# Two graph attention passes: ScalarE takes a share of the weighting of gathered rows

## The reference, cut to what matters

```python
def gatv2(x, src, dst, Wl, bl, Wr, br, att, bias, heads, out_ch):
    xl = (x @ Wl + bl).reshape(n, heads, out_ch)
    xr = (x @ Wr + br).reshape(n, heads, out_ch)
    e = jax.nn.leaky_relu(xl[src] + xr[dst], 0.2)
    score = jnp.einsum('ehc,hc->eh', e, att)
    smax = jax.ops.segment_max(score, dst, num_segments=n)
    ex = jnp.exp(score - smax[dst])
    denom = jax.ops.segment_sum(ex, dst, num_segments=n)
    alpha = ex / (denom[dst] + 1e-16)
    return jax.ops.segment_sum(xl[src] * alpha[:, :, None], dst, num_segments=n) ... + bias
x = gatv2(embed, ..., heads=4, out_ch=32)
x = jax.nn.relu(x)
return gatv2(x, ..., heads=1, out_ch=128)
```

## Time and profile before

| | us |
|---|---|
| median of three runs | 7670.53 |
| profiled execution, its own time | 7667.1 |
| span of the profiled execution | 7665.4 |
| passes 2 and 3, first gather to last add | 1126.9 and 1114.6 |
| pass 1, first gather to last add | 1079.1 |

### The profile page before, as it was taken

How to read it: one execution, slowest core, us unless ns; L and a number is a source line. 1 busy time by engine, 2 the same in 40 slices (tenths; PEclk the granted TensorE clock), 3 DMA queues, 4 the chain that set the end, 5 groups by cost and what they waited for, 6 DMA issues and landing times. The chain is left out here.

```text
span 7665.4 us, 88585 instructions
## 1 busy us (share of the span) xinstructions
PE 4650.8 (61%) x25719; PEld 3975.8 (52%) x25719; DVE 5099.6 (67%) x13667; ACT 1077.1 (14%) x3113; POOL 4877.5 (64%) x5168
## 2 busy tenths in 40 slices
PE   0444445566664467777567777776656677666665
PEld 0344443455553355555355555665555567555554
DVE  4333334577777788888688888647777754777776
ACT  0333332000000111111111111110000011000001
POOL 0777774677774577777377777137777702777771
PEclk8666666677776788888688888887777778777777
DMA  1444443666664344444344444456666635666662
GB/s 47 156 156 157 158 155 78 212 210 212 211 211 116 101 154 155 151 151 151 89 150 151 151 159 153 124 199 209 216 212 213 199 108 189 215 215 211 218 208 67
DMA packets 396877, 1264.71 MB, mean 165 GB/s; under 512 B 121860, under 2 KB 175678, under 8 KB 310014
## 3 DMA queue, kind: packets, MB, share of 16 engines
q1 hardware_dynamic: 195086, 766.00, 27.4%
q0 software_dynamic: 201328, 493.18, 22.6%
HBM read 1085.24 MB, written 173.47 MB: 164 GB/s over the span
## 5 line engine op out<-in xcount | busy, mean ns | idle before, releaser
L686 POOL DMA_INDIRECT gathered_rows<-table_l,gather_index x4176 | 4034.1, 966 | 1878.7 <-issue 1237.3
L1212 PE MATMUL ps<-weighted_rows,onehot 128*128 128x136 f32 (+2 forms) x8320 | 1603.0, 358 | 1333.4 <-DVE acc L1069 1330.6
L1212 PEld LDWEIGHTS ps<-weighted_rows,onehot 128*128 128x128 f32 x8320 | 1426.7, 256 | 1471.7 <-issue 834.6
L1179 PEld LDWEIGHTS ps<-dst_side,onehot_t 128*128 128x128 f32 x8320 | 1340.8, 238 | 337.8 <-issue 299.8
L1179 PE MATMUL ps<-dst_side,onehot_t 128*128 x8320 | 1407.6, 325 | 72.7 <-issue 45.3
L1069 DVE TENSOR_TENSOR acc<-acc,ps 128x136 f32 (+2 forms) x4160 | 1184.3, 285 | 108.8 <-PE ps L1212 8.2
L992 DVE TENSOR_REDUCE scores<-products 128x16 f32<-128x512 f32 (+2 forms) x1040 | 708.1, 681 | 13.4
L768 DVE TENSOR_TENSOR acc<-acc,ps 128x128 f32 x832 | 238.8, 287 | 692.0 <-PE ps L805 669.3
L686 POOL DMA_INDIRECT weights<-table_l,gather_index x612 | 579.7, 947 | 186.4 <-issue 174.8
L805 PE MATMUL ps<-gathered_rows,onehot 128*128 128x128 f32 x1664 | 352.6, 378 | 566.2 <-ACT gathered_rows L744 565.2
L1176 PE MATMUL ps<-gathered_rows,ident 128*128 128x512 f32 x832 | 540.4, 736 | 184.2 <-DMA gathered_rows<-table_l,gather_index 184.1
(11 more groups left out here) (286 smaller groups left out, 4741.6 us busy)
## 6 DMA issues: line engine op xcount, KB each, us to landing
onehot_t<-onehots_turned SPq DMA_DIRECT2D x260, 1024.0 KB
onehot<-onehots SPq DMA_DIRECT2D x260, 1024.0 KB, 5.1
gathered_rows<-table_l,gather_index POOLq DMA_INDIRECT x4176, 2.5
onehots<-onehot SPq DMA_DIRECT2D x52, 1024.0 KB, 6.9
onehots_turned<-onehot_t SPq DMA_DIRECT2D x52, 1024.0 KB, 4.3
table_l<-gathered_rows SPq DMA_DIRECT2D x50, 1024.0 KB, 4.4
segment_flags_sb<-segment_flags SPq DMA_DIRECT2D x1300, 8.2 KB
onehot<-type_mask_rows SPq DMA_DIRECT2D x50, 256.0 KB, 5.3
```

Of the source, the lines that this page charges most:

```text
L686: pool.indirect_dma_start(out=home(v, t // GC)[:, t % GC, :], out_offset=None, in_=table, in_offset=bass.IndirectOffsetOnAxis(ap=e.idx[:, ...
L1179: ins = nc.tensor.matmul(ps[:, BZ + k, g * P:(g + 1) * P], e.ohT[:, u, t * P:(t + 1) * P], kRows[:, bass.ds(bs[t % 8], D)], start=not gat, ...
L1212: ins = nc.tensor.matmul(ps[:, BP + n % 4, 256 * g:256 * g + PW], e.oh[:, u, t, :], exvT[:, t, :], start=True, stop=True)
```

## The change

In pass 2 ACT weighs chunk 3 of each group's four chunks, in pass 3 it weighs chunks 2 and 3. DVE keeps the other three and two. ACT has no instruction that multiplies a whole chunk by a factor that differs by tile and head; it scales one block by a value per partition. So `weigh_by_act` issues one ACTIVATE for each tile and head: 16 of 128x32 in pass 2 and 8 of 128x128 in pass 3, each with the exponential as its scale, read from SBUF. It stands in ACT's slot behind `keep_column` and ahead of the copy of chunk 2. A semaphore for each pass, `act_weighed`, counts the chunks that ACT has weighed. POOL waits for it before it overwrites such a chunk's rows, and TensorE before the sums that read it. `exv_ready` still counts four to a group: DVE's last `weigh` raises it by 1 + by_act.

```diff
+ACT_CHUNKS = {2: 1, 3: 2}
...
+        act_weighed = {no: Signal(sem(f"rows_weighed_by_act_{no}"), 0) for no in ACT_CHUNKS}
...
-                    free.wait(pool, pass_no - free_before, J * (s - buffers) + t // GC + 1)
+                    j = t // GC
+                    free.wait(pool, pass_no - free_before, J * (s - buffers) + j + 1)
+                    if j >= J - by_act:
+                        e.act_weighed[pass_no].wait(pool, 0, by_act * (s - buffers) + j - (J - by_act) + 1)
...
+    by_act = ACT_CHUNKS.get(no, 0)
+    by_dve = J - by_act
...
+            def weigh_by_act(s, v):
+
+                e.excol_ready.wait(act, a_no, s + 1)
+                for j in range(by_dve, J):
+                    for g in range(GC):
+                        t = GC * j + g
+                        for h in range(H):
+                            ins = nc.scalar.activation(exvH[:, t, h, 0:hs], home(v, j)[:, g, vrow + h * hs:vrow + (h + 1) * hs],
+                                                       ACT.Copy, scale=exvH[:, t, h, hs:hs + 1])
+                    ins.then_inc(e.act_weighed[no].sem, 1)
...
                     keep_column(s, u, q)
+                if weigh and by_act:
+                    weigh_by_act(s - 2, (w - 2) % buffers)
+                if cur:
                     keep_pair_sums(s, 2)
...
-                                bc(exE[:, GC * j:GC * (j + 1), :], hs), ALU.mult).then_inc(e.exv_ready.sem, 1)
+                                bc(exE[:, GC * j:GC * (j + 1), :], hs), ALU.mult).then_inc(e.exv_ready.sem, 1 if j < by_dve - 1 else 1 + by_act)
...
-                    for j in range(J):
+                    for j in range(by_dve):
                         weigh(p, vp, j)
...
+                if n % 2 == 0 and n // 2 >= by_dve:
+                    e.act_weighed[no].wait(pe, 0, by_act * s + n // 2 - by_dve + 1)
```

More of the change, by code:

```diff
@@ L246, in build @@
         env.rows_weighed, env.column_kept = rows_weighed, column_kept
+        env.act_weighed = act_weighed
         env.oht_made, env.oht_ready, env.onesF, env.p0_ready, env.p_ready = oht_made, oht_ready, onesF, p0_ready, p_ready
@@ L672, in static, with gather_rows @@
     return isinstance(s, int) and s < below
-def gather_rows(nc, e, block, pass_no, table, home, free, free_before, here, buffers, ways):
+def gather_rows(nc, e, block, pass_no, table, home, free, free_before, here, buffers, ways, by_act=0):
     @block.gpsimd
@@ L861, in attention_pass @@
     with nc.Block() as block:
-        gather_rows(nc, e, block, no, table, home, e.exv_ready, 1, here, buffers, ways)
+        gather_rows(nc, e, block, no, table, home, e.exv_ready, 1, here, buffers, ways, by_act)
         flags_base = [sum(16 * (h + 1) * ((NG + 1 - u) // 2) for h in (4, 4, 1, 8, 8)[0:a_no]) for u in range(2)]
```

## The result

The changed kernel took 7641.86 us (median of 6 runs, 7636.59 to 7648.16) beside 7670.24 for the kernel before (7663.92 to 7673.64): a ratio of 0.9965, 95% interval 0.9955 to 0.9975, or 28 us less. The forecast was 7626, with a range of 7603 to 7658. A second measurement, on another chip, gave 7657.85 beside 7677.49: 0.9971 [0.9962, 0.9981], 20 us less. The profiled execution after is the slowest of its six (7648.16 own time), so the two profiles differ by 19 us only; what follows works with their pass lengths.

A forecast was written before the change was run, and what follows sets the result against it. DVE's loop, with the four `weigh` on it, was taken to bound passes 2 and 3. Pass 2's -30 us and pass 3's -14 took 7667.1 to 7623; the median's 3.4 more gave 7626, range 7603 to 7658.

The forecast's parts named there:

- the bound and the price: Passes 2 and 3: DVE's loop sets the period, each `weigh` on it costs 0.62 us.
- ACT's work is hidden: ACT's weighing, 4 us a group in pass 2 and 2.5 in pass 3, fits a 9.5 us gap; 1 us charged.
- gathers take over in pass 3: Pass 3: DVE's loop falls to 1050 us, below the gathers' 1079, so POOL sets the pace; -14 us.
- Rival C: Passes 2 and 3: L985 stays at POOL's worst phase, 0.95 us lost a group; 7686 us; chance 0.07.
- the same four starts: L985's starts at 0, 3.0, 6.6 and 8.9 us, against POOL's 1.25 us steps: a quarter of phases costs nothing.
- Rival A: Passes 2 and 3: gathers at pass 1's pace, without loss beside L985; -32 and -35.5 us, 7603; chance 0.17.
- a shorter DVE loop in pass 2 asks for less, about 0.3: Pass 2: POOL's loss beside L985 shrinks with DVE's loop, from 0.7 to about 0.3 us a group.
- I take -30, since the collisions follow the loop: Pass 2's gain, set between -32 us by DVE's loop and -27 by gathers losing 0.4 a group.
- The chance value of 0.4: POOL's gathers: four L985 to a group, 0.1 us each by chance, lengthen issue by 0.4 us a group.
- the floor: Passes 2 and 3: the gathers' own pace taken as pass 1's 1079.1 us from first gather to last add.
- Added waits [...] nothing: POOL's wait on `act_weighed` costs nothing; TensorE's waits ahead of sums 4 and 6 are already met.
- -44 forecast: Passes 2 and 3 together: -30 us and -14 us against the profiled execution of 7667.1 us.

The follow-up runs named there:

- e5b: Kernel before, DVE weighing all chunks, with the leaky ReLU left in PSUM so L985 has one SBUF input: 7667.01 us beside 7677.49 (0.9985).
- e4c: Changed kernel with the leaky ReLU left in PSUM, so L985 has one SBUF input: 7618.55 us, 0.9924 of the kernel before.
- e7: Changed kernel with L985's input in PSUM, TensorE's waits for ACT moved earlier, and ACT weighing two chunks in both passes: 7614.26 us (0.9917).

## Why the prediction was right or wrong

**Right: the bound and the price.** DVE's loop with the four `weigh` on it bounded pass 2, 0.62 us each; after, three take 1.87 (2.47 before), and e5b shows the loop as the bound from the other side. The direction and the range held.

**Right: ACT's work is hidden.** Sixteen 128x32 took 3.49 us in a gap of 9.5, 0.22 each; I had 4.0. The Trainium skill's estimate of 3.4 by the formula of "ScalarE: Activation LUTs", section "What ACT_TABLE_LOAD costs", was the closer one, and its rule, to multiply on VectorE, had no price here when it was not followed. In pass 3 eight 128x128 took 126.59/52 = 2.4 us a group (2.5 forecast):
```profile
3739.00:4850.00 1111.00, 126.59 (x416) 0.83 0.45 149
```

**Right: gathers take over in pass 3.** POOL's busy time there was 812.28 (forecast 806 to 811, so just above). 1065.6 us from first to last gather against pass 1's 1042.8 is a loss of 0.44 a group (0.4 forecast). Rival C's phase of 0.95 did not come. (Laid over the same four starts again, about a fifth of the phases is free and not a quarter, which changes no term.) Rival A's case, no collisions, is what e4c makes: 59 us under the kernel before on that chip, where A had 67.

**The step that failed: "a shorter DVE loop in pass 2 asks for less, about 0.3", and so "I take -30, since the collisions follow the loop".** Pass 2 gave -15.7. I had treated POOL's losses as something that the loop asks for: while DVE was the bound that was right, POOL's loss equals its surplus of speed. But once the loop fell to 20.2 us by the median slot and 20.4 by the mean (e4c), 0.1 to 0.4 above the gathers' 20.05, no greater loss could hide behind it. POOL's lost time over pass 1 in pass 2 was 28 us (1070.9 - 1042.8), 0.54 a group, and 0.6 on the second chip. The chance value of 0.4 was the thing to carry into pass 2 as into pass 3, with its own scatter; then the gathers would have allowed -27 at best, as my sum noted and then passed over. e4c is the proof: without collisions the same kernel's pass 2 fell from 1118.7 to 1100.9 us, near the 1097 that I had given it with them. Three profiles of this pass with them took 1111.2, 1118.7 and 1115.2 us.

**Two terms mis-sized, and one that was not.** First, the floor. I took pass 1's whole 1079.1 us as the gathers' pace, but its tail isn't a GAT pass's. After the last gather of pass 3 come 41 us (4805.3 to 4846.3) where pass 1 has 36 (1078.6 - 1042.8), so the floor is 1043 + 41 = 1084, which e4c and e7 reach (1084.2, 1083.4). 5 us of pass 3's miss of 6 are this. Second, "Added waits [...] nothing": the second wait on sums 6 costs 0.07 us a slot, up to 3.6 us a pass. The price of a `weigh` on the loop was right: by the mean of pass 2's slots from 2800 us on, the loop took 20.97 us before and 20.42 in e4c, 0.55 less, which is 0.62 less the 0.07 of the wait. In the changed kernel, with collisions, it is 20.67.

The mean stands above the median (20.71 before, 20.2 after) because single slots are longer, one in seven before (22.1 to 22.2 us) and one in five after (21.7 to 23.1). Lines of a short and of a long slot, from the timeline after:
```profile
3443.13 1.12 PE L1198 MATMUL ps<-gathered_rows,ident 128*128 128x512 f32 x2
...
3463.72 2.07 PE L1198 MATMUL ps<-gathered_rows,ident 128*128 128x512 f32 x2
```
The second of them lies in this window (its us, busy of PE, PEld, DVE, ACT and POOL, granted clock, DMA share, GB/s):
```profile
3463.70:3466.70 3.00, 3.00 (x9) 1.94 (x9) 0.48 (x2) 0.00 (x0) 2.38 (x3) 0.52 0.76 227
```
The same two matmuls, the first of chunk 0 of the next group, take 2.07 us in place of 1.12 in the long slot, in a stretch whose granted clock is 0.52, the 1.2 GHz level, against 0.90 in the 20 us ahead of it. They stand between sums 6 and 7 and ACT's copy of chunk 0, on the loop. Of the nine slots over 21.5 us from 2800 us on in the changed kernel, eight have a granted clock of 0.50 to 0.68 in this place (the 4 us that end 0.5 us before the slot's end) and the ninth waits 6.5 us for a gather; in the slots of 20.2 us the clock there is 1.00. The two of 23.1 us have both the low clock and a wait for a gather. The kernel before and e4c have such slots too and lose as much by them (0.26 and 0.24 us a slot, mean less median; 0.46 in the changed kernel, its waits for gathers included), so the clock isn't what took the gain. Why it falls there wasn't tested.

**How the terms add up.** From -44 forecast to -24 in the two passes between the profiles: pass 2 fell short by 14 us, pass 3 by 6 (5 of it the floor). Of the 14, e4c puts some 4 on the loop itself (1100.9 against 1097, the second wait), and the other 10 are POOL's losses; e4c ran on another chip, so this split is an estimate. The rest of the distance is in pass 0 (+3.4) and in single us of the others, within what runs of one kernel differ by.

**The Trainium skill on who disturbs whom.** "SBUF — State Buffer", section "Who interferes with whom", infers that a VectorE instruction with two SBUF inputs leaves the issue of GpSimd's DMAs alone. The runs decide against it: 823.74 and 811.77 us of issue with two SBUF inputs, 792.46 and 789.87 with one of them in PSUM, and 39 us of the kernel's time.

**Open.** What holds up each group in all passes on some chips, and why the kernels without collisions are 2.4% to 3.1% slower than the kernel before there. That a POOL further ahead loads the same path more would fit, but no run tests it. Why a long gather ends 0.82 us after L985 isn't shown beyond the operand. Nor was it tried to shift the phase of POOL against L985.

## What to carry to other kernels

When a bound is taken away, give the next one the losses that it has by itself, not those that the old bound let through: an engine that was held in step by collisions brings them along when it takes over. Before moving work between engines, look for long instances of the next bound's instructions and what starts beside them; here that cost was larger than the one moved, and went with one operand. For a floor, use a pass of the same kind, its tail included.

## What the runs showed of the hardware

- A gather's issue on POOL takes 0.94 us, and up to 1.67 when it starts between 0.2 us before and 0.5 us after a DVE `tensor_tensor` with two SBUF inputs; those then end 0.82 us after that instruction's end (3399.75 + 1.30 against 3399.56 + 0.67), some 1.5 us after its start. With one input in PSUM it goes. A gather that starts 0.3 to 0.5 us ahead of such an instruction overlaps it too and takes its 0.94 us. I had expected only starts behind L985, and at most 0.5 us.
- A second semaphore wait on a matmul delays its weight load by 0.07 us (0.05 to 0.12 behind the last releaser, in all fourteen profiles, by whether the pass has this wait).
- One kernel took 7670 to 7678 us on three chips and 9730 to 10041 on three others, and the changed kernel with L985's input in PSUM took 0.9924 of its time on one of the first and 1.0314 of it on one of the others.
